# Four gated transformer layers on one core: ten blocks merged into one, steps in plain sequence, 22 chunks in layer 1

## What is computed

```
for l in 0..3:
    x = x + tanh(g_xattn[l]) * xattn_l(layernorm(x), ctx)
    x = x + tanh(g_ffn[l])   * ffn_l(layernorm(x))
```

## Time and profile before

| | |
|---|---|
| three runs | 1038.25, 1052.16 and 1039.94 us, median 1039.94 |
| the profiled execution, its own time | 1034.47 us |
| its span | 1032.70 us |
| TensorE, VectorE, ScalarE, GpSimd busy | 84%, 74%, 55%, 29% of the span |
| mean granted clock of TensorE | 0.92 |

### The profile page before, as it was taken

How to read it: one execution, slowest core, us unless ns; L and a number is a source line. 1 busy time by engine, 2 the same in 40 slices (tenths; PEclk the granted TensorE clock), 3 DMA queues, 4 the chain that set the end, 5 groups by cost and what they waited for, 6 DMA issues and landing times. The chain is left out here.

```text
span 1032.7 us, 17111 instructions
## 1 busy us (share of the span) xinstructions
PE 868.7 (84%) x5336; PEld 667.3 (65%) x5336; DVE 760.3 (74%) x1876; ACT 567.9 (55%) x1091; POOL 304.1 (29%) x495
## 2 busy tenths in 40 slices
PE   3899586798999997699999999689967679995695
PEld 2677464576666664477777777478845359984483
DVE  4799577579999995588788878678856445545686
ACT  2688253357777775366756665377734334442374
...
DMA packets 26069, 14.12 MB, mean 14 GB/s; under 512 B 11111, under 2 KB 25470, under 8 KB 25982
## 3 DMA queue, kind: packets, MB, share of 16 engines
...
HBM read 11.99 MB, written 1.05 MB: 13 GB/s over the span
## 5 line engine op out<-in xcount | busy, mean ns | idle before, releaser
L785 ACT ACTIVATE L_pt<-bank 128x512 f32<-128x512 f32 x224 | 127.2, 598 | 40.3 <-PE bank L660 26.5
L446 POOL TENSOR_TENSOR L_kc<-L_kc_all,const 128x256 fp32r<-128x256 f32 x96 | 58.8, 616 | 148.0 <-PE bank L660 73.6
L2187 DVE TENSOR_TENSOR L1f_h_lo<-L1f_h,L1f_h_hi 128x512 fp32r<-128x512 f32 (+1 forms) x96 | 84.1, 876 | 11.9 <-ACT L1f_h_hi L2084 11.8
L1969 POOL TENSOR_TENSOR L1f_xg_lo<-L1f_xg_raw,L1f_xg_hi 128x512 fp32r<-128x512 f32 x32 | 41.4, 1295 | 171.2 <-ACT L1f_xg_hi L2078 171.2
L2073 ACT ACTIVATE L1f_a<-bank 128x512 f32<-128x512 f32 (+1 forms) x96 | 57.3, 598 | 56.4 <-PE bank L2002 56.2
L917 DVE TENSOR_REDUCE L_ms<-bank 128x2 f32<-128x512 f32 x128 | 83.7, 685 | 4.0 <-PE bank L618 3.5
L772 ACT ACTIVATE L_part<-bank,L_bias_ca,const 128x256 fp32r<-128x256 f32 x128 | 68.8, 563 | 29.8 <-PE bank L595 28.7
L2182 DVE TENSOR_TENSOR L1f_h<-L1f_a,bank 128x512 f32<-128x512 f32 (+1 forms) x96 | 65.4, 681 | 26.4 <-ACT L1f_a L2073 21.4
L915 DVE TENSOR_REDUCE L_mc<-bank 128x8 f32<-128x512 f32 (+1 forms) x96 | 65.3, 681 | 6.5 <-PE bank L613 4.6
L2084 ACT CAST L1f_h_hi<-L1f_h 128x512 fp32r<-128x512 f32 (+1 forms) x96 | 59.2, 616 | 9.9 <-DVE L1f_h L2182 9.9
L618 PE MATMUL bank<-L_k,L_q 32*128 32x256 f32 x256 | 55.6, 340 | 8.6 <-DVE L_ms L917 5.4
...
## 6 DMA issues: line engine op xcount, KB each, us to landing
L_raw<-in_L_ffn_w_dram SPq DMA_DIRECT2D x8, 176.0 KB, 2.3
L_raw<-in_L_ffn_v_dram SPq DMA_DIRECT2D x8, 176.0 KB, 2.5
x<-in_x_dram SPq DMA_DIRECT2D x2, 512.0 KB, 5.6
...
mask<-in_mask_Bx1xSxS_ff_dram SPq DMA_DIRECT2D x2, 512.0 KB, 4.7
out_dram<-x SPq DMA_DIRECT2D x2, 512.0 KB, 4.0
...
```

The lines of the kernel that those rows point to most:

```text
L446: pool.tensor_tensor(kc[:, g], kc_all[:, g, bass.ds(b, 1)].bitcast(F32).to_broadcast([P, GH, S2]), pr.c("head4").unsqueeze(2).to_broadcast ...
L785: act.activation(pt[:, g // 2, (g % 2) * NS + (HEADS_1[i] if own_keys else i)], b_st[(g * NS + i) % 2][:], ACT.Exp, scale=scale).then_inc( ...
L2187: dve.tensor_tensor(h_lo[0:m, r], h[0:m, r], h_hi[0:m, r].bitcast(F32), ALU.subtract).then_inc(sem["lo_done"], 1)
```

## The change

- **One block.** Each function returns a `Stage` of an order and, per engine, the functions of its steps. `build` joins the orders with `weave` and an empty table `CUES`, so the program is their plain concatenation; semaphores are shared by name, and waits count from `past[...]`, what earlier stages raised. Nothing is cleared or met between stages. Tensors lie at fixed places (`layout`), and where a place or a PSUM bank is used again, the first user waits for the last reader.
- **Loads.** x comes in four transfers and leaves in four, each behind its own part of x. The loads of a later stage stand in SyncE's order of an earlier one.
- **Fronts of layers 0 and 3.** Rounds are written one behind the other; `route` has two parts of five steps, over 12 tiles and over 4, the second inside the loop behind `mul(0)` to `mul(4)`. Layer 3's products h, of which some stood among the routing's steps (L2598), are VectorE's part of `up` throughout.
- **Layer 1.** 22 chunks of 128 rows per block: six of them span two experts. Such a chunk takes ungated tokens for `u`, and its gates come by one more matmul (`rows`, with `sel_rows`) and one more VectorE product.
- **Layer 2.** All four rounds stand ahead of the loop.
- **Attention.** In layer 1 all `p_kc`, `p_vc` and `p_vg` stand ahead of the first sample. Statistics are aggregated in groups of four tiles, the later ones in the loop (`p_moments`, `p_rstd`). `attention3` fills one place of zeros instead of three.

```diff
-        with nc.Block() as block:
+    return Stage(order, sync, gpsimd, tensor, scalar, vector)
...
+CUES = {}
...
+        for stage in stages:
+            program = weave(program, of(stage, *stages[stage].order), *CUES.get(stage, ()))
...
+    ROUTED = (range(0, 3 * T), range(3 * T, NT))
+    order = [("load",), ("prepare",), ("zero",)]
+    for i in range(3):
+        order += [("moments", i), ("rstd", i), ("scale", i), ("turn", i), ("logits", i)]
+    order += [("route", 0, part) for part in range(5)] + [("up", 0), ("up", 1)]
+    order += [("moments", 3), ("rstd", 3), ("scale", 3), ("turn", 3), ("logits", 3)] + [("up", n) for n in range(2, AHEAD)]
+    order += [("gates", 0)]
+    for n in range(N):
...
+        order += [("gate", n), ("mul", n)]
+        if n < 5:
+            order.append(("route", 1, n))
...
+    order = [("weights", m) for m in range(3)]
+    for i in range(NI):
+        order += [("moments", i), ("rstd", i), ("scale", i), ("turn", i)]
+        if i == 1:
+            order += [("up", 0), ("up", 1)]
...
+            if k % C in SHARED:
+                x = shared_before(k)
+                dve.wait_ge(sem["rows_done"], past["rows_done"] + x + 1)
+                dve.tensor_tensor(h[:, r], factor, b_rows[:], ALU.mult).then_inc(sem["h_gated"], 1)
+                dve.wait_ge(sem["h_gated"], past["h_gated"] + x + 1)
+                factor = h[:, r]
...
-            for h in range(2):
-                sp.dma_start(ov[:, 8 * h:8 * h + 8], pr.x[:, 8 * h:8 * h + 8]).then_inc(stored, 16)
+        def put(k):
+            sp.wait_ge(sem["x_done"], past["x_done"] - NI + k + 1)
+            sp.dma_start(ov[:, T * k:T * k + T], pr.x[:, T * k:T * k + T]).then_inc(sem["stored"], 16)
```

4197 lines of the change are left out of this document (2076 added, 2121 removed).

## The result

| | |
|---|---|
| after, 4 runs | 1084.56 to 1086.69 us, median 1085.47 |
| before, 4 runs beside them | 1038.25 to 1052.16 us, median 1042.41 |
| ratio after / before | 1.04, 95% interval 1.0323 to 1.0477: slower |
| the profiled execution after, its own time and its span | 1085.97 and 1084.2 us |
| mean granted clock, after and before | 0.894 and 0.920 |

The forecast of 1058 us was too low by 27, and the time lies above the range's end of 1074; slower by over 2% had been given 0.43. The changed kernel takes 51.5 us more in its span than the one before. Where they arise is read from one kind of row: VectorE's update of x, `x<-bank,gates,x`, the last instruction of each stage on the data. Length here is from the end of a stage's last such row to that of the next. (Set-up counts to the first attention.)

What follows compares the result with a forecast made beforehand. No engine busy throughout: chains through all engines bound layers 0 and 3's feed-forward parts, TensorE layer 1's. Terms 16.5 + 14 + 5 − 7 − 4 + 0 − 2.5 = +22 on 1034.47 gave 1056.5, taken as 1058; range 1040 to 1074.

Steps and rivals of the forecast that it cites:

- Set-up and layer 0: 0, −2 to +3: Set-up and layer 0's attention: x in four pieces, later last statistics, later powers in the loop; 0 us, −2 to +3.
- The step on SyncE's loads: SyncE's queue: a waiting load holds those behind it, but each is needed only a stage later; costed at nothing.
- Layer 2: +1, −1 to +3: Layer 2's attention: +1 us, with bounds −1 to +3.
- Layer 3: −3: Layer 3's attention: power over four tiles instead of 16 and two memsets fewer; −3 us, −4 to −1.
- Layer 0's part, +16.5: Layer 0's feed-forward part: serial rounds, nine ups no longer free, second routing part in the loop; +16.5 us, +11 to +21.
- Layer 3's, +14: Layer 3's feed-forward part: serial rounds, four ups before gates 0, second routing part +2 in the loop; +14 us, +8 to +19.
- Layer 2's, +5: Layer 2's feed-forward part: four rounds ahead of the loop where one had been; +5 us, 0 to +9.
- Layer 1's, −7: Layer 1's feed-forward part: 22 chunks for 24 save TensorE time, 1.5 us taken back per block; −7 us, −12 to 0.
- Rival 2: Layer 1's feed-forward part: VectorE in shared chunks holds TensorE as much as is saved; +5 us, 1063; chance 0.10.
- Attention 1, −2; border and store: Layer 1's attention −2 us, an earlier projection; border waits inside other terms; last store −2.5, as only 256 KB remain.
- Rival 3: Stage borders: each of nine worth 3 us, not 1.1, so −17: 1041, no change, or about 1020; chance 0.13.
- Rival 1: Layers 0, 3, 2: low-clock ups, routing parts delaying products, rounds of 7.0; +13 us, 1071; chance 0.22.

Runs made afterwards that it cites:

- experiment 2: Changed kernel with the transfers of x and the gates issued ahead of the eight bias loads in set-up; 1080.04 us.
- experiment 1: Changed kernel with the later statistics and powers of attention 0, 2 and 3 moved from the loop to the front; 1078.89 us.
- experiment 9: Changed kernel with GpSimd's zeros for the gates in layers 0 and 3 placed behind the third round instead of first; 1087.83 us.
- experiment 3: Changed kernel with attention 2's front reordered: context products in banks 4 and 5, values' products behind the first projections, statistics earlier; 1080.73 us.
- experiment 6: Changed kernel with the second routing part of layers 0 and 3 moved from the loop to behind the fourth round's logits; 1076.51 us.
- experiment 11: Kernel of Experiment 10 with layer 3's first routing part alternating with ups, and the second part's steps after the exponential in the loop; median 1017.01 us.
- experiment 7: Changed kernel with layer 2's feed-forward rounds overlapped by one, next statistics and power ahead of each normalisation; 1078.15 us.
- Experiment 8: Changed kernel without VectorE's product by the rows' gates in layer 1's six shared chunks per block, that part of the result left out; 1084.12 us.
- experiment 4: Changed kernel with layers 0 and 3's rounds overlapped as in the kernel before, all routing ahead of the loop over the ups; 1046.4 us.
- experiment 5: Changed kernel with four serial rounds in layers 0 and 3, then both routing parts with all ups beside them; 1076.9 us.
- Experiment 10: Changed kernel with the edits of experiment 1, experiment 2, experiment 3, experiment 4 and experiment 7 together; median 1021.59 us, ratio to before 0.9827.

## Why the prediction failed

The miss is 29.5 us on the profiled spans (51.5 against 22 forecast). By the prediction's own steps:

- **"Set-up and layer 0: 0, −2 to +3"** failed: +7.4. The step saw that "x lands in four pieces but its last statistics later" and "later powers sit in the loop", and priced both at nothing. SyncE's order puts eight bias loads of 5.5 us ahead of x, where the kernel before had x first (experiment 2: 5 us), and the power in the loop holds the keys back (experiment 1: 2.8 to 5.0, of which 1.1 is the clock's). One more is a fill that ran early (1.1, experiment 9). The step on SyncE's loads, "each is needed only a stage later", had the same hole: x is needed at once. Together these are more than 7.4; part of that is the changed kernel's own execution, the longest in this stage.
- **"Layer 2: +1, −1 to +3"** failed: +10.6. Powers in the loop (3.9, experiment 1) and a projection behind the values' products of the same bank (4.9, experiment 3). I had not followed the banks of the order there; the table gave only the steps.
- **"Layer 3: −3"** was right in front, 47.3 to 44.0 for the first x, and blind behind it: two samples of 14.10 took 3.4 back. Experiment 1 gives 6.5 us for this stage: 3.3 of it from the two samples, and the first x 3.2 earlier again.
- The powers are one error in all three. What I wrote down for SyncE ("a load that waits holds those behind it") is what GpSimd's rows show at 71.05, and I did not put it to GpSimd, whose list `p_rstd` entered. The prediction should have asked, for each group of four tiles, what stands behind its power and who waits for that. The biases and the values' products are of the same kind: what is needed at once stands behind what is not.
- **Layer 0's part, +16.5**, came out as +18.3, and its steps are right almost one by one. Three rounds: 22.3 forecast, 21.9 measured; end of the first routing part 30.9 and 30.4 (its last row, `L0f_gx`, ends at 148.05); fourth round 37.9 and 37.4; its logits 0.8 and 1.8, as in this place they wait for the low half; nine ups 8.3 and 8.6; gates 0 at 47.0 and 47.8. The loop's share was +2 and is +3.0 (+2.8 by experiment 6).
- **Layer 3's, +14**, came out as +19.6. The mis-sized term is the second routing part: "+2 in the loop" measured +5.7 from gates 0 to the last x and 7.1 by experiment 6. About 2 of this are the exponential between two table loads of ScalarE, which the prediction had counted once, ahead of the first part; about 5 are the part's other steps (experiment 11). Gates 0 were 1.6 late: 1.0 for the logits as in layer 0, and 0.9 for the four ups, 8.4 instead of 7.5: twelve matmuls rather than ten at the lower clock and a gap of 0.5. The rounds and the first routing part ended 0.2 early.
- **Layer 2's, +5**, came out as +7.4. The last low half stands 29.9 behind x, 29.6 was forecast; the loop behind it took 32.6 instead of 30.5, and experiment 7 left it so. The chunks are not the reason, they follow each other at 2.27 us on the mean (2.2 to 2.3 was forecast); the mis-sized term is what lies around them: 3.5 from the last low half to the first `L2f_h_lo` and 4.1 from the last `L2f_h_lo` to the last x, where 3 had been allowed for.
- **Layer 1's, −7**: −8.2, by the step as written: 10.1 us less of TensorE and 1.9 more of idle time, where 1.5 per block had been feared. Experiment 8 shows that VectorE's new products are nearly hidden. Rival 2 was wrong.
- **Attention 1, −2; border and store**: −1.5, and −2.2 for −2.5. Rival 3, borders worth 3 us each, was wrong as far as it could be seen: by experiment 4 layer 0's front gains 2.0, with the load of the router in it. No experiment takes the other borders by themselves.
- **Rival 1, the sparse heads, 1071**: it was nearest to the time. Of its terms the routing parts in the loop came true (+4 forecast beyond the sum, +4.7 measured: 1.0 in layer 0, 3.7 in layer 3). The sparse heads by which it was named did not: the ups before gates 0 took 1.2 more than forecast, not 6.1, and layer 2's rounds 0.3, not 3. Together that is 6.2 of the 29.5, so its nearness is mostly luck: 20.6 lie in the attentions, which it left as they were.

**The clock, once more.** With more waiting the mean granted clock fell from 0.920 to 0.894, and layer 0's front ran at 0.54, layer 3's at 0.60. Between the levels 0.50 and 1.00 these means put 16% of the span before and 21% after at the lower one (an estimate from the two means); what that costs in time no experiment shows. The nine ups took 8.6 us, and the rows had given 8.3. By the rule of the Trainium skill ("TensorE: Matmul & The Clock Gate", Part 1: The HAM clock gate) they would have been 6.2. For these ups the trace does not agree with leaving the clock out. That it costs the whole kernel more than the Trainium skill's 1% is not shown: the 0.7% that the prediction held against that rule lies below it, as do the 2.4 us of the nine ups and the 8.2 us, 0.8% of the span, by which the tail of attention 1 was longer at 0.57 in experiments 1 and 5.

**Where the 51.5 us lie, by experiments** (each against the changed kernel): rounds and routing in layers 0 and 3 36.2 (experiment 4), powers in the loop 15.4 (1), layer 2's rounds 6.9 (7), layer 2's front 4.9 (3), x behind the biases 5 (2): 68.4, less what the change gained, 8.2 in layer 1 and some 9 in layer 3's attention front, borders, attention 1 and store. Experiment 10 had them all and measured 63.9, so they add up but for 4.5 us; 1 to 2 of those are attention 0 of the changed kernel's one profiled execution, which enters both experiments 1 and 2.
